# Bias and mask of query and key as one-row matmuls, and a new loop order, in a two-layer transformer kernel

## The reference

```python
x = x + _L0_xattn_ref(ctx, ctx, _layernorm(x), ssm_kernel, D, 8)     # long convolution of k times v, then times q
x = x + _L0_ffn_ref(_layernorm(x), gate_w, gate_b, ...)               # quantised gated product, 256 -> 1024 -> 256
x = x + _L1_xattn_ref(_layernorm(x), ctx, mask, mask, Wq, bq, ...)    # masked attention, 16 heads of 8 channels
x = x + _L1_ffn_ref(_layernorm(x), Wc, temperature, genes, ...)       # top 32 of 512, softmax, two small products
```

```python
q = jnp.einsum('oc,bct->bot', Wq, target) + bq[None, :, None]
k = jnp.einsum('oc,bcs->bos', Wk, source) + bk[None, :, None]
mask = target_mask[:, :, :, None] * source_mask[:, :, None, :]
dot = mask * (q . k / sqrt(8)) - (1.0 - mask) * NEG
```

## Time and profile before

| | |
|---|---|
| Median of 3 runs | 637.79 us (636.56 to 638.38) |
| The profiled execution's own time | 638.83 us |
| Its span in the profile | 637.0 us |
| Mean granted clock of TensorE | 0.918 of 2.4 GHz |

### The profile page before, as it was taken

One profiled execution on the slowest core, in us unless ns is written; L12 is line 12 of the kernel. 1 busy time (PEld: TensorE's weight loads), 2 busy tenths in 40 slices (PEclk: granted clock), 3 DMA queues, 4 the chain that ended last, 5 costly groups with the idle time before them and its releaser, 6 DMA issues.

```text
span 637.0 us, 11622 instructions
## 1 busy us (share of the span) xinstructions
PE 489.8 (77%) x3633; PEld 279.4 (44%) x3633; DVE 478.4 (75%) x885; ACT 341.0 (54%) x562; POOL 400.4 (63%) x711
## 2 busy tenths in 40 slices
PE   0264859898988588888899899899888887977543
PEld 0144646666766244434444444444444343433211
DVE  2446556888888868688999999999988778784441
ACT  0312642422122257667778777778856657675431
POOL 5629748878888655866787877876645454332232
PEclk9769898999988889899999999999989789897966
DMA  9654000002050625646535535634644635511100
GB/s 309 179 182 126 15 28 8 26 1 43 0 114 3 130 76 96 123 102 126 95 98 96 137 96 92 143 97 76 148 111 75 138 104 115 95 31 39 45 8 16
DMA packets 94243, 56.41 MB, mean 89 GB/s; under 512 B 14868, under 2 KB 93909, under 8 KB 94183
## 3 DMA queue, kind: packets, MB, share of 16 engines
q1 hardware_dynamic: 88692, 51.52, 36.0%
q10 hardware_dynamic: 5490, 4.16, 2.1%
HBM read 37.74 MB, written 19.52 MB: 90 GB/s over the span
## 4 chain that ended last, share of the span: by engine, by line
PE 21%; DVE 21%; issue 18%; DVEq 18%; POOL 10%; POOLq 5%; DMA 5%; ACT 2%; SPq 0%
PE pair L273 6%; DVE w_int L1495 4%; DVEq L1453 3%; PE bank L490 3%; DVEq L1536 3%; DVEq L1404 3%; DVEq L1546 2%; DVE prod L1357 2%; DVE best L1547 2%; POOL kv L872 2%; DVEq L1529 2%; DMA scr_toeps<-scr_toep 2%; DVEq L1432 2%; DVE st L1405 2%; PE pair L461 2%
## 5 line engine op out<-in xcount | busy, mean ns | idle before, releaser
L1495 DVE TENSOR_REDUCE w_int<-pair 128x4 f32<-128x1024 f32 x128 | 155.7, 1216 | 22.7 <-PE pair L461 22.3
L1219 ACT ACTIVATE cT<-pair 128x1024 f32<-128x1024 f32 x128 | 130.8, 1022 | 60.7 <-PE pair L477 59.1
L273 PE MATMUL pair<-kv,toep 128*128 128x256 f32 x384 | 104.7, 414 | 38.6 <-DMA toep<-scr_toeps 17.1
L273 PEld LDWEIGHTS pair<-kv,toep 128*128 128x128 f32 x384 | 74.6, 206 | 59.3 <-issue 22.5
L872 POOL TENSOR_TENSOR kv<-cT 128x512 f32<-128x512 f32 x64 | 66.1, 1039 | 30.7 <-PE pair L273 25.8
L461 PE MATMUL pair<-KS,w_raw 54*128 54x256 bf16 x512 | 52.5, 285 | 29.7 <-DVE w_int L1495 29.5
L490 PE MATMUL bank<-cT,v_aug 128*32 128x256 f32 x1024 | 72.9, 405 | 0.0
L1357 DVE TENSOR_TENSOR prod<-pair,qT 128x512 f32<-128x512 f32 x64 | 44.3, 692 | 37.2 <-PE pair L273 32.7
L477 PE MATMUL pair<-w_raw,KS 57*128 57x256 bf16 x512 | 52.5, 285 | 14.7 <-DMA w_raw<-w_int 6.4
L1364 DVE TENSOR_REDUCE yT<-prod 128x64 f32<-128x512 f32 x64 | 43.9, 686 | 6.2 <-issue 0.4
L461 PEld LDWEIGHTS pair<-KS,w_raw 54*128 54x128 bf16 x512 | 16.2, 96 | 73.4 <-DVE w_int L1495 60.1
(11 more groups left out here) (162 smaller groups left out, 990.2 us busy)
## 6 DMA issues: line engine op xcount, KB each, us to landing
w_raw<-scr_q SPq DMA_DIRECT2D x32, 192.0 KB
KS<-scr_k SPq DMA_DIRECT2D x32, 192.0 KB
scr_q<-w_int SPq DMA_DIRECT2D x16, 192.0 KB, 2.6
scr_k<-w_int SPq DMA_DIRECT2D x16, 192.0 KB, 2.6
scr_o<-qT SPq DMA_DIRECT2D x64, 36.0 KB
yT<-in_x SPq DMA_DIRECT2D x4, 512.0 KB, 8.4
ctx_all<-in_ctx SPq DMA_DIRECT2D x4, 512.0 KB, 10.2
x_b<-in_x SPq DMA_DIRECT2D x16, 128.0 KB, 5.1
```

The costliest lines, as they stand in the source:

```text
L273: mm = pe.matmul(bank[:, lh * n:(lh + 1) * n], toep[:, h, (lh - sh) * P:(lh - sh + 1) * P], rhs[:, sh, :], start=(sh == 0), stop=(sh == lh))
L1219: act.activation(probs[g % 4].rearrange("p j l -> p (j l)"), SC[:], ACT.Exp).then_inc(s("scores_free"), 1)
L1495: dve.tensor_reduce(neg_max[:, :, 2 * g:2 * g + 2].rearrange("p t j -> p j t"), M[:].rearrange("p (j t s) -> p j t s", t=KL, s=L), AX.X, A ...
```

## The change

It replaces VectorE's two bias and mask products. The masked x is made by a new product on GpSimd (`mask_x2`), the biases become two matmuls with one row (the bias times the mask, added in the bank), and a new step of ScalarE (`copy_qk`) copies the finished bank. The biases are loaded as rows.

```diff
@@ -99,7 +99,7 @@
         bv0 = sb("bv0", [P, C])
-        bqk = sb("bqk", [P, 2])
+        bqk_row = sb("bqk_row", [1, 2, C])
@@ -429,8 +429,11 @@
                 take6("qk", b)
-                pe.matmul(X6[:, L:2 * L], wqkvT[:, 1, :], ctx_m[b % 2][:], start=True, stop=True)
-                pe.matmul(X6[:, 0:L], wqkvT[:, 0, :], xn2, start=True, stop=True).then_inc(s("qk_bank_ready"), 1)
+                pe.matmul(X6[:, L:2 * L], wqkvT[:, 1, :], ctx_m[b % 2][:], start=True, stop=False)
+                pe.matmul(X6[:, L:2 * L], bqk_row[:, 1, :], mask_b[b % 2][0:1, :], start=False, stop=True)
+                pe.matmul(X6[:, 0:L], wqkvT[:, 0, :], xn2, start=True, stop=False)
+                pe.matmul(X6[:, 0:L], bqk_row[:, 0, :], mask_b[b % 2][0:1, :], start=False, stop=True
+                          ).then_inc(s("qk_bank_ready"), 1)
@@ -961,7 +964,15 @@
                     pool.wait_ge(s("qk_bank_ready"), b)
-                normalise(b, x2[:, b % 6, :], xn2, MEAN2, RSTD2, 1.0, LN_EPS, "xn2_ready")
+                normalise(b, x2[:, b % 6, :], xn2, MEAN2, RSTD2, 1.0, LN_EPS, "xn2_written")
+
+            def mask_x2(b):
+                if not live(b):
+                    return
+                k = b % 2
+                pool.wait_ge(s(f"ctx{k}_loaded"), 32 * (b // 2 + 1))
+                pool.wait_ge(s("xn2_written"), b + 1)
+                pool.tensor_tensor(xn2, xn2, mask_b[k][:], ALU.mult).then_inc(s("xn2_ready"), 1)
@@ -1081,7 +1093,7 @@
             for n, src in enumerate((a["bq"], a["bk"])):
-                act.dma_start(bqk[:, n:n + 1], src.rearrange("(p o) -> p o", o=1)).then_inc(s("small_in"), 16)
+                act.dma_start(bqk_row[:, n, :], src.rearrange("(o n) -> o n", o=1)).then_inc(s("small_in"), 16)
@@ -1192,6 +1204,14 @@
 
+            def copy_qk(b):
+                if not live(b):
+                    return
+                act.wait_ge(s("qk_bank_ready"), b + 1)
+                if b >= 1:
+                    act.wait_ge(s("qk_parts_ready"), b)
+                act.activation(qk.rearrange("p n l -> p (n l)"), X6[:], ACT.Copy).then_inc(s("x6_free"), 1)
+
@@ -1395,7 +1416,7 @@
             dve.tensor_scalar(temp_scale[:, 0:1], temp_scale[:, 0:1], 0.1, None, ALU.max)
-            dve.tensor_scalar(bqk[:, 0:1], bqk[:, 0:1], QK_SCALE, None, ALU.mult)
+            dve.tensor_scalar(bqk_row[:, 0, :], bqk_row[:, 0, :], QK_SCALE, None, ALU.mult)
@@ -1475,17 +1496,6 @@
 
-            def bias_and_mask_qk(b):
-                if not live(b):
-                    return
-                k = b % 2
-                dve.wait_ge(s("qk_bank_ready"), b + 1)
-                if b >= 1:
-                    dve.wait_ge(s("qk_parts_ready"), b)
-                dve.scalar_tensor_tensor(qk[:, 1, :], mask_b[k][:], bqk[:, 1:2], X6[:, L:2 * L], ALU.mult, ALU.add)
-                dve.scalar_tensor_tensor(qk[:, 0, :], X6[:, 0:L], bqk[:, 0:1], mask_b[k][:], ALU.add, ALU.mult
-                                         ).then_inc(s("x6_free"), 1)
-
```

More of the change, by code:

```diff
@@ new lines, in _ @@
+            for m in range(B + 11):
+                maxima(m - 7, 0)
+                gate(m - 2, 0)
+                transpose_maxima(m - 8)
+                later_convolve(m - 3, 9)
+                project_v(m - 7)
+                value(m - 2, 0)
+                later_convolve(m - 2, 0)
+                maxima(m - 7, 1)
+                logits_product(m - 10)
+                gate(m - 2, 1)
+                scores(m - 8, 0)
+                transpose_y(m)
+                later_convolve(m - 2, 1)
+                later_convolve(m - 2, 2)
+                value(m - 2, 1)
+                maxima(m - 7, 2)
+                scores(m - 8, 1)
+                later_convolve(m - 2, 3)
+                projection_weights(m - 1)
+                transpose_xq(m - 1)
+                transpose_weights(m - 11)
+                maxima(m - 7, 3)
+                scores(m - 8, 2)
+                later_convolve(m - 2, 4)
+                project_qk(m - 5)
+                scores(m - 8, 3)
+                maxima(m - 7, 4)
+                values(m - 8, 0)
+                scores(m - 8, 4)
+                expressed(m - 11)
+                maxima(m - 7, 5)
+                scores(m - 8, 5)
+                down_up(m - 11)
+                values(m - 8, 1)
+                later_convolve(m - 2, 5)
+                maxima(m - 7, 6)
+                scores(m - 8, 6)
+                ffn_product(m - 3)
+                values(m - 8, 2)
+                scores(m - 8, 7)
+                maxima(m - 7, 7)
+                choice_weights(m - 2)
+                later_convolve(m - 2, 6)
+                later_convolve(m - 2, 7)
+                out_weights(m)
+                transpose_hidden(m - 2)
+                values(m - 8, 3)
+                later_convolve(m - 2, 8)
+                transpose_xr(m - 9)
@@ new lines, in _ @@
+            for m in range(B + 11):
+                later_query(m - 3, 8)
+                top_strike(m - 11, 3)
+                later_sum(m - 3, 8)
+                open_gate(m - 2, 0)
+                later_query(m - 3, 9)
+                statistics_x2(m - 4)
+                maxima(m - 7, 1)
+                inverse_weight_sum(m - 11)
+                later_sum(m - 3, 9)
+                later_query(m - 2, 0)
+                top_first(m - 10)
+                later_sum(m - 2, 0)
+                first_sum(m)
+                open_gate(m - 2, 1)
+                later_query(m - 2, 1)
+                maxima(m - 7, 2)
+                inverse_denominators(m - 9)
+                later_sum(m - 2, 1)
+                top_strike(m - 10, 0)
+                later_query(m - 2, 2)
+                maxima(m - 7, 3)
+                later_sum(m - 2, 2)
+                statistics_x1(m)
+                later_query(m - 2, 3)
+                later_sum(m - 2, 3)
+                top_next(m - 10, 1)
+                maxima(m - 7, 4)
+                later_query(m - 2, 4)
+                later_sum(m - 2, 4)
+                hidden_scales(m - 2)
+                maxima(m - 7, 5)
+                top_strike(m - 10, 1)
+                top_bias(m - 10)
+                top_next(m - 10, 2)
+                later_query(m - 2, 5)
+                maxima(m - 7, 6)
+                later_sum(m - 2, 5)
+                second_sum(m - 3)
+                statistics_x3(m - 9)
+                down_times_up(m - 11)
+                maxima(m - 7, 7)
+                later_query(m - 2, 6)
+                top_strike(m - 10, 2)
+                later_sum(m - 2, 6)
+                scale_x(m)
+                later_query(m - 2, 7)
+                top_next(m - 10, 3)
+                later_sum(m - 2, 7)
+                maxima(m - 6, 0)
```

249 lines of the change are left out of this document (75 added, 174 removed).

## The result

The changed kernel is slower: 650.71 us median of four executions (647.4 to 658.91) against 638.09, a ratio of 1.021 (1.015 to 1.026). The forecast was 633 us, with 645 as its upper end. Built again for the experiments it took 653.96 us, 1.022 (1.017 to 1.027). The profiled execution is the longest of the four, 658.91 us with a span of 657.1. It is one of the slow executions that a kernel has now and then, so its profile shows where time went, while its 20.1 us over the profile before are more than the 12.6 us between the medians.

What follows compares the result with a forecast made beforehand. VectorE was taken to bound the seven periods from 280.47 to 450.92, a ring of engines the late ones. 638.83 - 5.5 - 2 + 2.6 = 633.9, 633 us against the 637.79 median; range 623 to 645, the forecast's own 630 to 636.

Steps and rivals of the forecast that it cites:

- The one-row matmuls: TensorE's two added bias matmuls per batch: 0.44 us each, 0.88 together, bounded by a full matmul of two 0.438 us passes.
- TensorE's margin in the steady stage: Steady stage: TensorE's work rises to 22.96 us per batch, 1.0 us below VectorE's 23.99, so VectorE's gain stands.
- The early stage: First two periods with a query split: GpSimd's product costs 0.73 us, VectorE gives 0.78; together nothing, 1.5 us either way.
- VectorE's 5.5 us: Seven VectorE-bound periods, 280.47 to 450.92: removing two products saves 0.78 us each, 5.5 us in all.
- its sign of being wrong: Steady period above 24.4 us, where 24.0 was expected, or first convolution after the prologue still starting at 97.4.
- rival (b): Steady stage: GpSimd's new product disturbs VectorE's denominator product, losing some 0.4 of 0.78 us per batch; 635.8 us, chance 0.08.
- Late stage, -2 us: Four periods, 450.92 to about 545: between +1.6 and -3.0 us a batch, taken as -0.5, -2 in all.
- The tail: Last batches' chain of weights, transposes and down product: order between engines unchanged, so costed at nothing.
- Rival (d): A several-engine ring already bounds the steady stage, adding 0.83 us to each of 11 periods; 649.5 us, chance 0.18.
- this ring: Transposed maxima, reload, context load and product, new product, projection, scores, maxima; the prediction saw a several-engine ring after 450.
- The order, costed at nothing but the bias loads: Whole kernel: drains, TensorE's refills and the projection's later place cost nothing; only SyncE's later bias loads cost time.
- SyncE's bias loads, +2.6 us: Start: 12 bias DMAs issued later delay the first gate product from 94.9 to 97.5, 2.6 us once, ends 1.5 and 4.

Runs made afterwards that it cites:

- the seven kernels: The seven profiled kernels with one-row matmuls, the changed kernel among them; their four late periods take 95.1 to 104.8 us, against 85.4 to 93.5 in the eleven others.
- the two versions with ScalarE's activations: Two ScalarE activations add the bias per partition, no added matmuls or mask product, query and key unmasked: new order 636.42 us (0.999), old order 631.72 us (0.988).
- the zeros: Kernel before plus two matmuls with a zero weight in the query and key projection: one row 657.17 us (1.031), 128 rows 642.08 us (1.008).
- the best version: Kernel before, its order kept, with two ScalarE activations adding the bias instead of VectorE's two products, query and key unmasked: 631.72 us, 0.988.

## Why the prediction was wrong, point by point

**The one-row matmuls: the step that failed.** The prediction took "0.44 us each, 0.88 together", and said they were "not above a full matmul of the same columns". They took 0.63 each, 1.3 us together with what they do to their neighbours. The upper bound left out the switch of rows. A sign of it could be read in the weight loads of the kernel before, which the prediction did not look at:

```profile
322.49 0.11 PEld L461 LDWEIGHTS pair<-KS,w_raw 54*128 54x128 bf16 x4 [0.76 <-DVE w_int L1495]
322.81 0.11 PEld L382 LDWEIGHTS bank<-wgvT,ctx_all 128*128 128x128 bf16 x2 [0.21 <-issue]
...
359.68 0.21 PEld L477 LDWEIGHTS pair<-w_raw,KS 57*128 57x128 bf16 x4
360.10 0.30 PEld L543 LDWEIGHTS bank<-wduT,exprT 128*128 128x128 f32 x2 [0.21 <-issue]
...
376.61 0.30 PEld L432 LDWEIGHTS bank<-ctx_m,wqkvT 128*128 128x128 f32 x2 [0.21 <-POOL ctx_m L971]
376.93 0.41 PEld L433 LDWEIGHTS bank<-ctx_all,wqkvT 128*128 128x128 f32 x2
```

From 54 or 57 rows to 128 the loader idles 0.21 us for "issue", also where both are bf16, so it isn't the change of type; from 128 to 128 in L432 and L433 it doesn't idle. What a switch to one row costs stood in no row. So a bound from matmuls that follow their own kind did not cover an operation that switches. The Trainium skill, "TensorE: Matmul & The Clock Gate", "Step-by-step: what each phase is for", says that weights are loaded ahead of running matmuls if the row groups don't conflict or the load goes to the background buffer, and that the row count does not matter for the time of a load. The trace agrees on that time (0.29 us for the one-row pair, 0.30 for the 128-row pair) and, from 128 to 128 rows, on the loading ahead (no idle time); between 1 and 128 rows the load was never ahead in any of the seven kernels.

The place of the cost was wrong too. The sum compared 0.88 with TensorE's margin in the steady stage, and the steady stage did swallow the matmuls: its period is 24.57 us with one row, 24.58 with 128 and 24.57 without. Outside it they cost 10 to 15 us in the new order and about 30 in the old, where the sum had nothing for the early stage and a gain for the late one. The early stage was costed at "nothing, with 1.5 us either way", with GpSimd and VectorE in view and TensorE left out, although the row showed TensorE busy for 21.69 us beside GpSimd's 21.96 (163.22 to 187.77). That window is not cut at the bias products, as the prediction says; between the first two of these the two engines are busy for 21.23 and 21.27 of 23.90 us. 8.9 us were lost by the first milestone. Part of this began with the order: in every profiled kernel with the new order the second projection starts at 199.4 to 203.8 us, against 193.2 before. The three new-order kernels without bias matmuls have made most of it up by the first milestone (256.8 to 257.9, against 255.3); the changed kernel has not.

**VectorE's 5.5 us.** The removal was right (0.78 us a batch). The steady period of 24.57 is above the 24.4 that the prediction had named as its sign of being wrong. What rival (b) described, with a chance of 0.08, took half of the gain back, as it had said:

```profile
386.87 0.74 POOL L975 TENSOR_TENSOR ctx_all<-ctx_all,mask_b 128x256 f32<-128x256 f32 x1
...
387.50 0.34 DVE L1516 RECIPROCAL den<-den 128x32 f32<-128x32 f32 x1
387.55 2.50 POOL L952 TENSOR_TENSOR w_raw<-w_raw 128x512 f32<-128x512 f32 x2
...
387.92 0.96 DVE L1518 TENSOR_TENSOR den<-den,mask_all 128x32 f32<-128x32 f32 x1
```

The mask product pushes the gate product onto the denominator product, which takes 0.96 us instead of 0.57. The sum 24.77 - 0.78 + 0.39 = 24.38 lacks 0.19 of the 24.57 measured. The new order without a mask product leaves the same remainder: there the denominator product takes 0.28, 24.77 - 0.78 - 0.29 = 23.70, measured 23.89. So 0.2 us belongs to the new order; it was not traced to an instruction. In the old order there is none: 24.77 - 0.78 + 0.68 = 24.67 with a denominator product of 1.25, measured 24.66. The rule of the Trainium skill, "SBUF — State Buffer", "SBUF: two separate sides", on the shared port thus bore on one instruction a batch and not on each new product; here the prediction had argued rightly. The price of the mask product outside the steady stage was missed: alone it costs 9 us in the old order, of which three steady periods explain 0.7 each.

**Late stage, -2 us.** It went the other way: in its four periods the milestones moved from 10.3 us late (449.9 to 460.2) to 16.3 (540.7 to 556.9), 1.5 a batch, next to the worse end of +1.6. The tail, costed at nothing, added 3.4 more. The step that failed here is again the matmuls: without them, with the mask product and the copy still in place, the four periods take 90.0 us against 90.8 before, and with them 96.7. At 1.2 GHz the four take 4.26 us (from 483.71) where the two of the kernel before take 2.0, so they add 2.3 and not "twice" 0.88. The waits that went from VectorE came back on GpSimd. Rival (d) had this ring as the bound and gave 649.5, close to the 650.7 measured, but by luck: it had the ring in the steady stage, where it is not, and it priced the matmuls at 0.88.

**The order, costed at nothing but the bias loads.** With the old arithmetic it costs 1.2%, and 1.1% between the two versions with ScalarE's activations, about 7 us. The 0.2 us in each steady period and the 1.5 us at the first gate product are a small part; where the rest arises was not traced.

**SyncE's bias loads, +2.6 us.** Right in place, and the time was nearly right: the first gate product was forecast at 97.5 and started at 97.03. The size was not: with the loads early it starts at 95.56, so the loads' place costs 1.5 us of the 2.6. Whether it is caught up later, as the run with the early loads hints, is below what its intervals resolve.

**The range.** Its upper end of 645 was made from the bounds of the terms. It took the bound on the one-row matmuls as firm, though no row showed such a matmul, and it left out any loss in the early stage and any from the order.

## What to carry to other kernels

A matmul with one row is not cheap filler: where it stands between 128-row ones, each switch lays a weight load open. Padding it with zero rows saved 6 to 8.5 us in the changed kernel, 15 with the zeros in the untouched kernel and 23 in the old order. Adding the bias where the bank is read anyway is cheaper still (the best version does). Work that is free in the steady stage of a pipeline can be paid in its ramp and tail, so cost it for every stage with the engine that sets that stage's pace. An order of steps fits its arithmetic: the new order is better by 2.9% with the one-row matmuls and worse by 1.1% with the ScalarE version.

## What the runs showed that was not expected

The same VectorE product of 128 x 32 takes 0.19 us alone and 0.28, 0.39, 0.57, 0.96 or 1.27 us in the steady stages of these kernels, by when it starts against GpSimd's pair of products of 2.5 us. In the kernel before it could be brought from 0.57 to 0.39 without a gain that the runs could show.

Two one-row matmuls a batch, with nothing in them, cost 3.1% of this kernel; the same two with 128 rows cost 0.8%.
